# One loop of steps for projection, attention and routing, with scores from float32r halves of heads in row pairs

## The reference, cut to what matters

```python
x = x + attn(layernorm(x))
    # c_kv = x @ W_DKV; k = c_kv @ W_UK; v = c_kv @ W_UV; q = x @ W_UQ
    # probs = softmax(causal(q k^T / 4)); ctx = probs v; ctx @ W_O
...
logits = layernorm(x) @ Wr / temp          # top 2 of 8, softmax over the two
h = xf @ W1[e] + b1[e]; a, g = split(h)
out += (a * silu(g) @ W2[e] + b2[e]) * we  # we: weight of expert e for the token
```

## Time and profile before

| | us |
|---|---|
| median of the runs | 1204.11 |
| span of the profiled execution | 1240.9 |

### The profile page before, as it was taken

One profiled execution on the slowest core, in us unless ns is written; L12 is line 12 of the kernel. 1 busy time (PEld: TensorE's weight loads), 2 busy tenths in 40 slices (PEclk: granted clock), 3 DMA queues, 4 the chain that ended last, 5 costly groups with the idle time before them and its releaser, 6 DMA issues. The chain is left out here.

```text
span 1240.9 us, 19607 instructions
## 1 busy us (share of the span) xinstructions
PE 1069.9 (86%) x5364; PEld 554.3 (45%) x5365; DVE 787.0 (63%) x2352; ACT 491.9 (40%) x1043; POOL 390.4 (31%) x721
## 2 busy tenths in 40 slices
PE   6897599999999999998587553089999999999995
PEld 2443123333333333332176543046666666666663
DVE  5654599999999999894057443245555555555553
ACT  2333047777777777777501212012122122122121
POOL 2224513333333333333403235512222222222222
PEclk9878569999999999999987565589999999999998
DMA  2665974444466644400266641212232232232232
GB/s 91 208 189 188 199 157 104 122 113 113 116 141 135 132 82 79 80 20 30 66 220 193 225 124 68 103 39 44 46 50 42 45 49 42 44 49 42 44 49 25
DMA packets 102396, 121.22 MB, mean 98 GB/s; under 512 B 26352, under 2 KB 81776, under 8 KB 102320
## 3 DMA queue, kind: packets, MB, share of 16 engines
q1 hardware_dynamic: 89024, 102.55, 32.5%
q0 software_dynamic: 13296, 17.77, 8.6%
HBM read 70.27 MB, written 49.63 MB: 97 GB/s over the span
## 5 line engine op out<-in xcount | busy, mean ns | idle before, releaser
L640 ACT ACTIVATE b_prob<-b_prob_ps 128x512 f32<-128x512 f32 (+3 forms) x768 | 318.0, 506 | 103.2 <-PE b_prob_ps L684 101.2
L596 DVE CUSTOM_DVE_ANT_0 b_max_ps<-b_max_ps,b_mask_max 128x384 f32<-128x384 f32 (+3 forms) x512 | 246.7, 503 | 50.4 <-PE b_max_ps L666 47.9
L666 PE MATMUL b_max_ps<-b_k_st,b_q_st 96*128 96x512 bf16 (+3 forms) x768 | 253.5, 345 | 24.2 <-DMA b_k_st<-k_parts 21.8
L684 PE MATMUL b_prob_ps<-b_q_st,b_k_st 99*128 99x512 bf16 (+3 forms) x768 | 239.5, 330 | 10.5 <-ACT b_prob L640 6.6
L554 POOL TENSOR_SCALAR_AFFINE_SELECT b_prob<-b_prob 128x128 f32<-128x128 f32 x512 | 146.6, 292 | 308.6 <-ACT b_prob L640 300.9
L1352 POOL DMA_INDIRECT out_dram<-e_y,e_token x71 | 110.1, 1551 | 326.1 <-DVE e_y L1406 310.4
L599 DVE TENSOR_REDUCE b_neg_max<-b_max_ps 128x1 f32<-128x512 f32 x256 | 176.1, 688 | 5.1 <-PE b_max_ps L666 2.6
L666 PEld LDWEIGHTS b_max_ps<-b_k_st,b_q_st 96*128 96x128 bf16 x768 | 74.4, 99 | 202.0 <-DVE b_neg_max L596 110.1
L703 PE MATMUL b_acc_ps<-b_prob,b_v_aug 128*32 128x512 f32 (+3 forms) x1536 | 163.4, 498 | 0.2 <-POOL b_prob L554 0.2
L1459 PE MATMUL e_g_ps<-w_sb,e_rowsT 128*128 x284 | 135.5, 600 | 0.3 <-issue 0.3
L1459 PE MATMUL e_a_ps<-w_sb,e_rowsT 128*128 x284 | 134.0, 594 | 0.0
(11 more groups left out here) (164 smaller groups left out, 1093.4 us busy)
## 6 DMA issues: line engine op xcount, KB each, us to landing
w_sb<-in_L_ffn_W SPq DMA_DIRECT2D x11, 1024.0 KB, 11.3
e_rows<-slot_rows SPq DMA_DIRECT2D x72, 129.0 KB, 2.1
ctx_cols<-b_ctx_out SPq DMA_DIRECT2D x16, 512.0 KB
q_parts<-a_part_q SPq DMA_DIRECT2D x8, 768.0 KB, 3.8
k_parts<-a_part_k SPq DMA_DIRECT2D x8, 768.0 KB, 4.2
b_q_st<-q_parts SPq DMA_DIRECT2D x16, 384.0 KB, 5.0
b_k_st<-k_parts SPq DMA_DIRECT2D x16, 384.0 KB, 7.7
a_x<-in_L_attn_x SPq DMA_DIRECT2D x8, 512.0 KB, 6.5
```

The costliest lines, as they stand in the source:

```text
L596: nc.vector.tensor_tensor_reduce(scores, scores, mask_max[:, HALF - width:HALF], -1.0, -MASKED, ALU.add, ALU.min, to).then_inc(max_done, 1)
L640: nc.scalar.activation(prob[n % NP][:, 0:width], prob_ps[n % NS][:, 0:width], ACT.Exp, scale=SCALE).then_inc(prob_ok, 1)
L666: nc.tensor.matmul(out[:, 0:width], q_st[g % RING][0:STACK, h, i * P:(i + 1) * P], k_st[g % RING][0:STACK, h, half * HALF:half * HALF + wi ...
L684: nc.tensor.matmul(prob_ps[n % NS][:, 0:width], k_st[g % RING][0:MAXROWS, h, j * P:(j + 1) * P], q_st[g % RING][0:MAXROWS, h, q0:q0 + widt ...
```

## The change

- The three phases ahead of the experts become one `fused_phase` with a loop of steps from -48 to 260. A batch of 4 quads has 48 steps. The projection of batch b+1 (chunks at slots 6 to 14 and 17 to 25 of the 48) and the routing of batch b-1 (from slot 20 to slot 65) are worked off inside the steps of batch b. The projection of batch 0 stands ahead, and the routing of batch 3 behind.
- Everything that is not scores or products shares one PSUM bank, `aux_ps`: TensorE fills it at the end of a step, ScalarE copies it at the beginning of the next, and only then may TensorE fill it again. The accumulated context has one bank in place of two; a different order of blocks finishes the first half before the second begins.
- Q and k are split into two float32r parts (GpSimd: a copy and a subtraction), so that three products are 48 contraction rows, and 50 with the two parts of the maximum. Two heads share a tile, one at partition 0 and one at 64. A prob block takes the head of the other half than the max block beside it.
- Inverse roots are taken by GpSimd as a power; normalising, the scaling of the context and the residual go to GpSimd. The softmax sum is spread to 128 partitions by a DMA through DRAM in place of matmuls. The diagonal blocks of a unit are zeroed in one instruction.
- The stacks of scores and the expert weights no longer fit together: the weights are loaded by ScalarE's queue once the last product is done. Biases are loaded in the expert phase, and the rows of a tile by ScalarE, two tiles ahead; TensorE waits there for the weights of each tile's expert.

```diff
-PARTS = 3
-RUNS = [(0, 0, 3), (3 * HD, 0, 2), (5 * HD, 0, 1)]
-STACK = 6 * HD
+PARTS = 2
+ROW_TILE = 64
+STACK = 3 * HD
+Q_RUNS = [(0, 0, 1), (HD, 0, 2)]
+K_RUNS = [(0, 0, 2), (2 * HD, 0, 1)]
...
+CHUNK_AT = [6, 17]
+SPREAD_AT, ADD_AT, NORMAL_AT = 26, 28, 37
+ROUTER_AT, COUNT_AT, SCATTER_AT = 42, 46, 50
...
+def halves_of(h):
+
+    return h % 2 * ROW_TILE, h // 2
...
-                nc.tensor.matmul(out[:, 0:width], q_st[g % RING][0:STACK, h, i * P:(i + 1) * P],
-                                 k_st[g % RING][0:STACK, h, half * HALF:half * HALF + width],
+                nc.tensor.matmul(out_ps[:, 0:width], q_st[g % RING][at:at + STACK, j, i * P:(i + 1) * P],
+                                 k_st[g % RING][at:at + STACK, j, half * HALF:half * HALF + width],
                                  start=True, stop=True).then_inc(max_sc_ok, 1)
...
+            def split(chunk, j):
+                n = 2 * DC * chunk + j
+                pool.wait_ge(aux_copied, project_aux(chunk, QK_STEP + j) + 1)
+                pool.wait_ge(part_st[j % 2], 16 * (n // 2))
+                nc.gpsimd.tensor_copy(part[j % 2][:, 0, :], raw[j % 2][:]).then_inc(hi_ok, 1)
+                pool.wait_ge(hi_ok, n + 1)
+                nc.gpsimd.tensor_tensor(part[j % 2][:, 1, :], raw[j % 2][:], part[j % 2][:, 0, :].bitcast(F32),
+                                        ALU.subtract).then_inc(lo_ok, 1)
...
+            def project(chunk, k):
+                if project_aux(chunk, k):
+                    pe.wait_ge(aux_copied, project_aux(chunk, k))
...
+            def load_weights():
+                act.wait_ge(prob_sc_ok, TOTAL * QUAD)
+                act.wait_ge(pv_ok, TOTAL)
+                for e in range(EXPERTS):
+                    act.dma_start(w1_sb[:, e, :, :], w1[e].rearrange("(c p) n -> p c n", p=P)).then_inc(w_in[e], 16)
+                    act.dma_start(w2_sb[:, e, :, :], w2[e].rearrange("(f p) n -> p f n", p=P)).then_inc(w_in[e], 16)
...
+            for s in range(-PERIOD, LAST):
+                if turned_at(s) is not None:
+                    max_rows_transposed(turned_at(s))
...
+                for n in range(s * QUAD, (s + 1) * QUAD):
+                    if 0 <= s < TOTAL:
                         max_scores(n)
+                    if 0 <= s - LEAD < TOTAL:
                         prob_scores(n - LEAD * QUAD)
+                if 0 <= s - LEAD - LAG < TOTAL:
+                    products(s - LEAD - LAG)
+                if at_chunk(s, 0, CHUNK_STEPS):
+                    project(*at_chunk(s, 0, CHUNK_STEPS))
+                if at_route(s, ADD_AT, PAIRS):
+                    heads_added(*at_route(s, ADD_AT, PAIRS))
```

More of the change, by code:

```diff
@@ L1435, in step @@
                     hidden_turned(n - 1, c - 1)
+            for n in range(AHEAD):
+                load(n, n)
             steps(act, step)
+            for n in range(SLOT_TILES, TABLE):
+                act.wait_ge(rows_ok[n % B], (n // B + 1) * 16)
         @block.tensor
```

1667 lines of the change are left out of this document (804 added, 863 removed).

## The result

The changed kernel is slower: 1408.5 us median (1401.6 to 1422.5, 4 runs) against 1206.4 (1200.9 to 1212.5) in the same series. The ratio is 1.168, 95% interval 1.162 to 1.174. The forecast was 1178 with 1105 to 1260, so it missed both the direction and the range. The profiled execution has a span of 1408.1 us. In all that follows the ratios leave out a run that took over 1.5% more than the shortest of its kernel; the profiles of e2, e4 and e6 are of such runs, and the ratio of e9 rests on two runs.

The account below looks back on a forecast made before the run. Attention was taken as bound by nearly full TensorE and VectorE, routing by its engine-to-engine chain, experts by TensorE. Terms summed to 1185 against 1240.9 us; without 30 us of unrecorded waits 26 less, so 1178 us, range 1105 to 1260.

Parts of the forecast that it names:

- the change part by part: The forecast's list of stage times for the whole kernel: 70 + 545 + 35 + 103 + 432 = 1185 us, against 1240.9.
- Plain steps, 2.1 us: Attention steps without other work: TensorE needs 1.9 us, less than VectorE's 2.09, so a step takes 2.1 us.
- One cycle a column: Score matmuls in attention: float32r was taken to stream one column per cycle, as one of a float32 matmul's four products.
- Steps with a chunk, 3.15 us: Attention steps with projection inside: TensorE 2.97 us plus a 0.2 us gap, 18 such steps per batch.
- Steps with routing: Attention steps with routing inside: heads 3.95 us and transposes 2.6 us, four times each; router 3.8 us, twice.
- Start, tail steps, experts: Stages outside the 192 steps and last routing: first max block at 70 us, 18 tail steps 35, experts 432.
- Last routing, 103 us: Routing of batch 3 behind attention: 197.8 us becomes 103, with 11 added for weight loads alongside; bounds 90 and 135.
- the tail eats it: Rival on last routing: weight issues hold up ScalarE and small transfers crawl, 133 in place of 103, 1208 us; chance 0.13.
- The 30 us of unrecorded waits: Routing of the kernel before: about 30 us of the profiled span, mostly absent from unprofiled runs, so not saved there.
- Scores at two cycles a column: Rival in attention: float32r streams like a float32 pass, 60 us more, 1238; chance 0.22, plus 0.05 for near 1500.
- Nearly free overlap: Rival in attention: gaps stay closed and loads hide behind the other row group, attention 490 us, whole 1123; chance 0.2.
- would show it: Profile signs listed for right (such as 48 plain steps in about 100 us) and wrong (such as TensorE waiting for maximum rows).

Follow-up runs that it names:

- e2: Changed kernel with the overlap taken out: all projection ahead of attention, all routing behind it; 1515.2 us, ratio 1.254 to the kernel before.
- e4: Changed kernel plus two unread 512-column bfloat16 matmuls ahead of the fourth max block, in steps without auxiliary work for five steps; 1414 us, ratio 1.168.
- e6: Kernel of e2 with max and prob block of the same head, so on the same rows of the array; 1713 us, ratio 1.374.
- e9: Changed kernel with expert weights issued by SyncE behind the last spread of inverse sums, instead of by ScalarE after the last product; median 1390.7 us, ratio 1.142.
- e5: Kernel of e2 with score operands read as bfloat16; 1453 us, ratio 1.169 on a chip where the kernel before took 1244.
- e7: Changed kernel with only the projection taken out of attention, all chunks ahead; 1455.7 us, ratio 1.168 on a chip where the kernel before took 1244.
- e13: Kernel of e7 (projection ahead, routing of three batches inside attention) with score operands read as bfloat16; 1409.0 us, ratio 1.169.
- e3: Changed kernel with the eight products issued ahead of the fourth pair of score blocks instead of behind it; 1411 us, ratio 1.172.
- e12: The kernel before, unchanged, profiled again on the chip of the other runs of its call; 1204.7 us, profiled span 1202.9.
- e10: Changed kernel with every part of a routing three steps later, loads of heads and rows left in place; 1424.0 us, ratio 1.182.
- e11: Kernel of e5 with max and prob block of the same head, so on the same rows of the array; 1488.6 us, ratio 1.235.

## Why the prediction was wrong, point by point

**The clock, which the sum left out.** This is the step that failed. Each term of "the change part by part" inside attention was priced at the high clock because attention before ran at 0.96; no term, rival or bound had the clock of attention in it. It was 0.75. e2 and e5 show the first cause: float32r scores bring it down with nothing else in the loop (0.81 against 0.94 in the profiles, and 0.50 against 0.88 on the same rows; e2 and e6 are there in their longest runs, and e2's others are 58 us over e5). e7 and e13 show the second: routing inside brings it down whatever the type (0.81 to 0.76, and 0.94 to 0.81). Why either does so stays open. Low steps cost about 1 us in 3.4 (3.40 against 2.40 in e2), so the 355 us at the low level cost some 105 of the 168.5 us that attention missed by.

**Where attention's 276 us are** (435 to 711). float32r alone 75 (e2 minus e5, by profiles). Work put inside, at the high clock: chunks 54 x 1.42 = 77, heads 12 x 1.65 = 20, transposes 12 x 0.94 = 11, router 6 x 2.4 = 14, together 122. Waits over 0.9 us 37. Low clock beyond e2's, 160 us of time at 0.29, 47. These make 281. With e2's other runs float32r alone is about 50 and the last term about 70, and the sum stays. The work and the low clock are estimates from step times and overlap a little; the sum of the overlap itself is measured, 201 by e2's profile and 227 with bfloat16.

**Plain steps, 2.1 us.** Mis-sized: 2.27 with bfloat16, 2.40 with float32r. "A float32 load at 0.11 to 0.12 us" was the spacing of loads in a row, while a load lasts 0.19 us in the earlier trace rows; a float32r load lasts 0.185, twice bfloat16's 0.093. By spacing the price was not too low: pairs of 128 columns, two loads each, start 0.16 us apart at the closest in e2 (0.07 in e5). "One cycle a column" held: at the low clock pairs of 512-column blocks start 0.43 us apart at the closest, and the row groups did start together; at the high clock it is 0.24 at the closest and 0.33 in the median. In the step shown above the four pairs take 1.77 us, 0.50 of it the wait, where 0.9 was forecast. I took the fuller VectorE as the bound of the step, and didn't ask what happens when TensorE hurries ahead of it: with three banks the fourth block waits 0.4 to 0.5 us, TensorE stands with the products behind it, and VectorE then stands for the products.

**Steps with a chunk, 3.15 us.** 3.82. The auxiliary part was near (the four passes of one q step in 1.98 us, where four of 0.43 were forecast). A good part of the missing 0.67 us is the same bank wait, which I had assumed to vanish in a longer step; after 2.5 us of products and projection VectorE starts each step empty. e3 moved it and won 0.34 us.

**Steps with routing.** Heads 3.95 forecast, 4.07 measured in the seven at the high clock and 6.8 in the other five; transposes 2.6 and 3.34; router 3.8 and 6.6, since the router's steps run at the low clock, where its weight loads take 0.33 us for 0.19. Late rows behind SyncE's large transfers were in none of the sums. What the auxiliary matmuls' third way of tiling the array costs in these steps no run tells apart.

**Start, tail steps, experts.** 70 and 74.5; 35 and 50.2 (at clock 0.64, while the earlier trace rows had 1.00); 432 and 433.5.

**Last routing, 103 us.** 136, past the bound of 135. The mechanism was named (weights beside the chain's small transfers) and mis-sized: I added 11 us, e9 gives 26 back. The rival "the tail eats it" had 133 and was right in its own stretch: ScalarE was held by its issues from 838 to 874 and GpSimd waited 49 us for the spread. The rule of the Trainium skill cited there (DMA: Bandwidth & Descriptors, Queues, rings and completion order) gave an estimate of 13 us; e9 against the changed kernel shows more, 25 us in the first wait alone.

**The 30 us of unrecorded waits.** Right in size (37, e12), right that the unprofiled runs of 1204 lacked them; profiling was the wrong reason. The changed kernel's span and median don't differ.

**The rivals.** "Scores at two cycles a column" pointed to the other side with the right suspect, but by the rate of columns, which was as forecast. "Nearly free overlap" is refuted even with bfloat16. No case had the price of the new form of projection and routing: e2 shows 306 us of rebuilding against 104 us of overlap won.

**What "would show it".** Right as forecast: the first block, blocks starting together, DMA full behind the last product. Shown wrong: 48 plain steps in 100 us (109 in e5, 128 in e2), 28 to 30 us for the nine steps of a chunk (33 to 39), and two of the alarms listed came up, waits for maximum rows and, in e10, for GpSimd's mask.

## What to carry to other kernels

Before work is put into a loop in which TensorE is full, price the loop at both levels of the clock, and ask of each new operand type and each kind of small matmul whether the loop keeps the high one; here it was a good part of the loss, and TensorE's busy share didn't show it. An overlap is paid for twice, by the work it puts into the full loop and by what the moved parts give up to fit: time the moved parts apart, as in e2, before believing the gain. And where the same kernel takes 3% more on another chip, compare versions by the stages of their traces, not by ratios to it. A late small transfer is not cured by another place in the program: each of three places had another engine's queue behind it.

## What the hardware showed that was not expected

- With float32r score matmuls of 48 rows, one behind the other, TensorE stayed at 1.2 GHz for 697 us while it was busy 99% of the time (e6's profile); the same blocks in bfloat16 ran at 0.94 in steps 48 to 143 and in pairs at 1.00 (e11, e5).
- A float32r weight load of 128 columns took 0.185 us at the high clock, a bfloat16 one of the same rows 0.093.
- The kernel before took 1200 to 1214 us in four series and 1236 to 1249 in two; its profiles at 1202.9 and 1240.9 differ by 37 us in the routing alone, where the longer one has the unrecorded waits.
- Twelve megabytes on a second hardware queue, started beside a chain of small transfers instead of behind it, delayed that chain by 25 us (e9).
